# Decoder on one core: the projection's add taken earlier in three attention stages, with the order of divide, raw sums and their inverse changed in two of them

## The reference, cut to what matters

```python
x = x + L0_attn(layernorm(x), ...)     # 16 heads of 8, causal; biases, LoRA
x = x + L0_xattn(layernorm(x), ctx)    # 16 heads, 'trinity' mask; biases
x = x + L0_ffn(...)
...
x = x + L2_attn(layernorm(x), ...)     # 16 heads of 8, causal, rotary embedding, no biases
...
x = x + L3_xattn(layernorm(x), ctx, ctx, mask, ...)   # 16 heads, mask read from memory
#   ctx_ = softmax(q k^T + mask) v per head; relu(ctx_ @ wo.T + bo)
x = x + L3_ffn(...)
```

## Time and profile before

| | us |
|---|---|
| median of 3 runs | 1747.38 (1746.98 to 1747.76) |
| profiled execution, its own time | 1735.4 |
| span of the profiled execution, first to last instruction | 1733.7 |
| TensorE busy (matmuls) | 1339.4 |
| VectorE busy | 946.9 |
| ScalarE busy | 918.7 |
| GpSimd busy | 400.3 |
| mean granted clock of TensorE, share of full speed | 0.879 |

### The profile page before, as it was taken

How to read it: one execution, slowest core, us unless ns; L and a number is a source line. 1 busy time by engine, 2 the same in 40 slices (tenths; PEclk the granted TensorE clock), 3 DMA queues, 4 the chain that set the end, 5 groups by cost and what they waited for, 6 DMA issues and landing times. The chain is left out here.

```text
span 1733.7 us, 27918 instructions
## 1 busy us (share of the span) xinstructions
PE 1339.4 (77%) x9137; PEld 827.9 (48%) x9137; DVE 946.9 (55%) x3708; ACT 918.7 (53%) x2185; POOL 400.3 (23%) x490
## 2 busy tenths in 40 slices
PE   5888888868899999777996888765083577878574
PEld 3455555545444444553564555454062444444464
DVE  4577767754455555444112776647223657666432
ACT  2688877762477766532421666732020467767232
POOL 4433333210311110100004332101544042210134
PEclk9899989999999999877998898886596879989687
DMA  7900000000000000000005000000222000000012
GB/s 207 141 2 2 2 2 1 2 1 1 1 1 1 1 1 1 1 1 1 1 1 179 1 1 2 1 1 12 61 69 79 1 19 13 12 8 1 10 58 78
DMA packets 60263, 42.34 MB, mean 24 GB/s; under 512 B 13188, under 2 KB 54120, under 8 KB 60120
## 3 DMA queue, kind: packets, MB, share of 16 engines
q1 hardware_dynamic: 54752, 32.42, 7.9%
q0 software_dynamic: 3552, 7.33, 1.2%
q10 hardware_dynamic: 1816, 0.81, 0.2%
HBM read 25.88 MB, written 14.66 MB: 23 GB/s over the span
## 5 line engine op out<-in xcount | busy, mean ns | idle before, releaser
L792 ACT ACTIVATE L0a_e<-L0a_e,L0a_neg_max 128x256 f32<-128x256 f32 (+1 forms) x512 | 190.6, 447 | 19.4 <-DVE L0a_neg_max L868 19.4
L679 PE MATMUL L0a_psE<-ident,L0a_e 128*128 128x128 f32 x768 | 121.9, 288 | 16.8 <-DVE L0a_probs L877 8.2
L1216 DVE CUSTOM_DVE_ANT_0 L3x_e<-L3x_psS,L3x_mask_rows 128x256 f32<-128x256 f32 x256 | 92.9, 420 | 64.3 <-PE L3x_psS L1076 64.3
L679 PEld LDWEIGHTS L0a_psE<-ident,L0a_e 128*128 128x128 f32 x768 | 86.9, 145 | 70.5 <-issue 35.9
L1164 ACT ACTIVATE L3x_e<-L3x_e,L3x_neg_max 128x256 f32<-128x256 f32 x256 | 110.7, 503 | 12.7 <-DVE L3x_neg_max L1216 12.7
L792 ACT ACTIVATE L2a_e<-L2a_e,L2a_neg_max 128x128 f32<-128x128 f32 (+1 forms) x256 | 95.2, 445 | 33.6 <-DVE L2a_neg_max L868 33.6
L1084 PE MATMUL L3x_psE<-ident,L3x_e 128*128 128x128 f32 x512 | 81.9, 292 | 28.2 <-DVE scores_L_experts_L L1226 13.8
L868 DVE CUSTOM_DVE_ANT_0 L2a_e<-L2a_psS,causal_rows 128x128 f32<-128x128 f32 (+1 forms) x256 | 76.1, 353 | 36.9 <-PE L2a_psS L669 31.5
L868 DVE CUSTOM_DVE_ANT_0 L0a_e<-L0a_psS,trinity 128x128 f32<-128x128 f32 (+1 forms) x256 | 75.1, 352 | 37.3 <-PE L0a_psS L669 33.3
L868 DVE CUSTOM_DVE_ANT_0 L0a_e<-L0a_psS,causal_rows 128x128 f32<-128x128 f32 (+1 forms) x256 | 75.3, 352 | 35.2 <-PE L0a_psS L669 31.6
L568 POOL TENSOR_SCALAR L0a_km<-L0a_kT,quad_rows 128x256 f32<-128x256 f32 x64 | 57.9, 922 | 155.2 <-ACT L0a_kT L785 155.2
(11 more groups left out here) (652 smaller groups left out, 3231.7 us busy)
## 6 DMA issues: line engine op xcount, KB each, us to landing
L2f_rows<-packed_rows SPq DMA_DIRECT2D x8, 325.0 KB
packed_rows<-zeros SPq DMA_DIRECT2D x1, 2560.0 KB, 30.3
experts_L_L<-in_L_ffn_w_dram SPq DMA_DIRECT2D x1, 2048.0 KB, 8.4
unpacked_rows<-zeros SPq DMA_DIRECT2D x1, 2048.0 KB, 19.9
scores_L_experts_L<-in_L_ffn_w_dram SPq DMA_DIRECT2D x1, 2048.0 KB, 7.8
L2f_back_rows<-unpacked_rows SPq DMA_DIRECT2D x16, 128.0 KB, 2.5
L3x_mask_rows<-in_mask_Bx1xSxS_ff_dram SPq DMA_DIRECT2D x8, 256.0 KB, 2.7
sorted_rows<-zeros SPq DMA_DIRECT2D x1, 1472.0 KB, 19.7
```

The source lines that it names most:

```text
L679: last = nc.tensor.transpose(psE[i % 2][:, c * P:(c + 1) * P], e[:, i % RING, c * P:(c + 1) * P], mem.ident[:])
L792: last = nc.scalar.activation(at, at, ACT.Exp, bias=neg[:, i % RING, j:j + 1], scale=-1.0)
L1216: last = nc.vector.tensor_tensor_reduce(out=e[:, i % RING, j * S:(j + 1) * S], in0=psS[r][:, j * S:(j + 1) * S], in1=mrow[:, b % 2, t, :], ...
```

## The change

1. quad_heads, VectorE: `settle_x(b)` keeps only the add of the projection (and still signals s_x); it moves from n = 3 to n = 2. The statistics become `measure_x(b)`, at n = 3. 
2. masked_heads, VectorE: `settle_x(b)` keeps only the add of projection and bias into proj, signals a new semaphore s_taken, and moves from n = 3 to n = 1; TensorE's `weigh(b-1, 0)` waits for s_taken instead of s_x. The relu and the add to x, with the statistics, are `measure_x(b)` at n = 3. Before it writes proj again, settle_x waits for s_x of the bank before.
3. quad_heads: keep_raw moves from n = 7 to n = 6 (VectorE), spread_sums from n = 6 to n = 5 (TensorE), invert from n = 8 to n = 7 (ScalarE). At even n = 8 ScalarE's order was exponent(8), keep(6), invert; now it is exponent(7), invert, exponent(8), keep(6).
4. quad_heads with rope (L2a alone), GpSimd: divide(b-1) stands ahead of variants(b+2) and behind combine(b+2). L0a keeps its order.

```diff
                 for b in range(NB):
+                    if b + 2 < NB and rope:
+                        combine(b + 2)
+                    if b > 0 and rope:
+                        divide(b - 1)
                     if b + 2 < NB:
-                        if rope:
-                            combine(b + 2)
                         variants(b + 2)
                     if biased:
                         add_bias(b)
-                    if b > 0:
+                    if b > 0 and not rope:
                         divide(b - 1)
...
-                        if n == 6 and b > 0:
+                        if n == 5 and b > 0:
                             spread_sums(b - 1)
...
-                    if n == 8 and b > 0:
+                    if n == 7 and b > 0:
                         invert(b - 1)
...
                     nc.vector.tensor_tensor(xb, xb, psO[:, 0:S].rearrange("p (t d) -> p t d", t=TPB), ALU.add).then_inc(s_x, 1)
+
+                def measure_x(b):
                     dve.wait_ge(s_x, b + 1)
...
+                    if n == 2 and b >= 2:
+                        settle_x(b - 2)
                     if n == 3 and b >= 2:
-                        settle_x(b - 2)
+                        measure_x(b - 2)
...
-                    if n == 7 and b > 0:
+                    if n == 6 and b > 0:
                         keep_raw(b - 1)
...
@@ masked_heads
                         if b >= 1:
-                            pe.wait_ge(s_x, b)
+                            pe.wait_ge(s_taken, b)
...
                 def settle_x(b):
                     dve.wait_ge(s_out, b + 1)
                     dve.wait_ge(s_rows_kept, 1)
+                    if b >= 1:
+                        dve.wait_ge(s_x, b)
+                    nc.vector.tensor_tensor(proj[:], psO[:, 0:S].rearrange("p (t d) -> p t d", t=TPB),
+                                            out_bias[:].unsqueeze(1).to_broadcast([P, TPB, D]), ALU.add).then_inc(s_taken, 1)
+
+                def measure_x(b):
                     xb = mem.x[:, b * TPB:(b + 1) * TPB, :]
-                    steps.step(nc.vector.tensor_tensor(proj[:], psO[:, 0:S].rearrange("p (t d) -> p t d", t=TPB),
-                                                       out_bias[:].unsqueeze(1).to_broadcast([P, TPB, D]), ALU.add))
+                    dve.wait_ge(s_taken, b + 1)
                     nc.vector.scalar_tensor_tensor(xb, proj[:], 0.0, xb, ALU.max, ALU.add).then_inc(s_x, 1)
...
+                    if n == 1 and b >= 2:
+                        settle_x(b - 2)
                     if n == 3 and b >= 2:
-                        settle_x(b - 2)
+                        measure_x(b - 2)
```

More of the change, by code:

```diff
@@ L923, in _ @@
                 settle_x(NB - 2)
+                measure_x(NB - 2)
                 keep(LAST - 3)
@@ L927, in _ @@
                 settle_x(NB - 1)
+                measure_x(NB - 1)
 def masked_heads(nc, mem, w, name, *, wo, bo, dram_mask, probs_at):
@@ L964, in masked_heads @@
         s_raw, s_den, s_ln, s_rec = sem("raw_ready"), sem("sums_spread"), sem("log_ready"), sem("reciprocal_ready")
-        s_yT, s_out, s_x = sem("yT_ready"), sem("out_done"), sem("x_done")
+        s_yT, s_out, s_taken, s_x = sem("yT_ready"), sem("out_done"), sem("projection_taken"), sem("x_done")
         chain = sem("dve_chain")
@@ L1247, in _ @@
                         keep(i - 4)
+                    if n == 1 and b >= 2:
+                        settle_x(b - 2)
                     if n == 3 and b >= 2:
-                        settle_x(b - 2)
+                        measure_x(b - 2)
                 settle_x(B - 2)
+                measure_x(B - 2)
                 keep(LAST - 3)
@@ L1253, in _ @@
                 settle_x(B - 1)
+                measure_x(B - 1)
 def stick_heads(nc, mem, w, name, *, wq, wk, wv, wo, probs_at, scale):
```

## The result

The changed kernel takes **1664.29 us** (median of 4 runs, 1663.35 to 1666.49), the kernel before beside it 1747.47 (4 runs, 1746.98 to 1747.76): a ratio of 0.9526, 95% interval 0.951 to 0.9543, 83 us less. Predicted were 1671.7, range 1659 to 1711. (Ratios here are of the runs that were compared with each other; they can differ by 0.2% from the quotient of two medians.) The profiled execution took 1666.49 us, its span is 1664.8: 69 us less than the profiled one of before.

A forecast was written before the change was run, and what follows sets the result against it. No engine is full, so order and waits bound the kernel. Savings of 23.8 (L0a), 28.7 (L2a) and 23.2 us (L3x) sum to 75.7, about 36 waits and 40 clock; from 1747.4 that gives 1671.7 us, range 1659 to 1711.

The forecast's parts named there:

- The cycle of L0a: L0a: a loop over TensorE, ScalarE and VectorE sets bank length; banks 2 to 9 fall from 18.93 to 18.67 us.
- The price of part 3: L0a, ScalarE: the inverse ahead of item 8 costs 1.17 us on the cycle, about 0.95 from bank 10 on.
- The clock: TensorE in L0a, L2a, L3x: gaps of 2 us also lower its clock; removing them returns 40 us.
- The rule that I weighed against it: TensorE: short idles between matmul groups can still make the clock go back and forth, so its 40 us stay lost.
- Rivals B: All three stages: TensorE's clock stays as it is, only 36 us of waits go; 1711 us, chance 0.17.
- C: L0a: the new 1.4 us gap at turn 8 lowers the clock as before; about 1693 us, chance 0.15.
- D: TensorE's clock stays low for whole banks, about 13 us each; slower, 1802 us at 10 banks, chance 0.05.
- Rival E: VectorE's earlier add meets an unfinished project and holds up reduces, losing settle_x's gain; about 1725 us, chance 0.05.
- L2a: Stage L2a: earlier add and divide, inverse free; banks of 18.91 us, 28.7 us saved, 10.3 of it clock.
- L3x: Stage L3x: the weigh's 2.14 us wait goes whole; banks of 22.4 us, 23.2 us saved, some 10.4 of it clock.
- The carry: Whole kernel: the median stands 12 us above the profiled execution, so 1659.7 us becomes 1671.7 us.

The follow-up runs named there:

- Filling the gaps alone: Kernel before, order and waits unchanged, with useless matmuls on TensorE in the gaps ahead of first weighs and L2a's project: 1698.64 us, ratio 0.9769.
- Part 1 alone: Kernel before with only quad_heads' add moved to n = 2, the statistics staying at n = 3: 1659.65 us, ratio 0.9693.
- parts 3 and 4 alone: Kernel before with only the moves of keep_raw, spread_sums and invert and GpSimd's earlier divide: 1742.26 us, ratio 1.0006.
- the add at n = 1, no part 3: Changed kernel with keep_raw, spread_sums and invert moved back and quad_heads' add at n = 1: 1604.79 us, ratio 0.9372; run again, 1604.55 us, ratio 0.9373.

## Why the prediction was right

**The cycle of L0a** held to 0.04 us in all but bank 14: banks 2 to 9 took 18.64 (18.67 predicted), 10 to 13 18.24 (18.28), bank 14 17.67 (18.0). The 13 banks from 95.69 to 335.53 came to 239.84 us (240.5). The weigh waits 0.55 and turn 8 1.40, as stated.

**The price of part 3** was right: 1.17 us on the cycle predicted, 1.15 measured twice, with and without the 0.55 us gap. What I did not draw from it is that the kernel would be better without: I counted it as a term of the sum and did not ask what it bought in L2a, which the runs show to be nothing.

**The clock** was right, and it was the step with the most at stake. Filling the gaps alone took off 40.2 us in the three stages (17.1 in L0a, 10.5 in L2a, 12.6 in L3x, where the sum had 19, 10.3 and 10.4). The rule that I weighed against it (the Trainium skill, TensorE: Matmul & The Clock Gate, "A second HAM failure mode: psum-queue depth-cycling"), by which short idles would keep the clock going back and forth, is not what these banks show: with a gap of 1.40 us, one of 0.52 and one of 0.55 in each bank the granted clock was 1.00 from 75 to 350. In the same windows of the kernels that kept a gap of 1.98 us or more it was 0.86 to 0.93. The idle time of a bank in all does not tell them apart either: in bank 3 of L0a TensorE's gaps of over 0.15 us add up to 2.44 us before and to 2.46 after. It is the one long gap that has gone. Rivals B and C fall by the windows, D with them: no score of 2.09 us is left amid banks 2 to 14 of L0a. Rival E falls too: VectorE's add waits for project in none of those banks, only at the end of a stage. What in the chip tells the ones from the others no run here settles; bank 2 of the earlier trace rows, full at a gap of 1.99, is not explained by the gap's length alone.

**L2a** gave 27.8 us (28.7): banks of 18.90 (18.91), bank 6 of 17.73. By parts, 17.2 of it hang on part 4 (207.1 against 189.9), though parts 3 and 4 together, with part 1 absent, gave 10.2 only. Part 1 alone and parts 3 and 4 alone each took the stage to 207.5, all together to 190. My sum by waits would have shared it out otherwise. One reason is the clock: only together do they remove all gaps of 2 us and more. The other is that the waits overlap: a bank took 22.08 us with its gaps filled, at best 21.46 with part 1 alone and 20.34 with parts 3 and 4 alone, but 18.90 with all.

**L3x** gave 24.4 us (23.2), banks of 22.35 (22.4).

**What was mis-sized.** In L0a I had -23.8 and found -20.6. The banks are as said; the difference is the stage's two ends, which the sum had put at nothing. From the first score to the first weigh of bank 1 it took 23.8 us after and 21.3 before, because the granted clock stayed at the low level for longer (a turn at 63.98 took 1.09 us after, one at 64.69 took 0.63 before), and from the first weigh behind the last bank to the end 10.1 us after and 8.9 before. The start is not the change's doing: bank 1's weigh comes ahead of every operation that was moved, and two runs of one kernel (the add at n = 1, no part 3) took 21.3 and 23.3 us for the same stretch.

The median fell by 83.2 us, the profiled execution by 68.9, the three stages in it by 72.8 (the others were 4 us longer after). I had said that the profiled execution of before stood 12 us under its median and carried the same step over: 1659.7 to 1671.7. The profiled execution came at 1666.5, 7 us above its forecast and 2 above its median, and the median 7 us below its own. So the near hit of the median is in part luck, as two errors of opposite sign stand in it. The carry was wrong: those 12 us most likely belong to the thing that the change removes, though no slow execution of the kernel before was traced to show it. The stage code of before, run again in other kernels, took 360.2 instead of 355.2 us in L0a and 225.7 instead of 221.6 in L3x, by the clock behind the same gaps. The profiled execution seems to have been a lucky one, and a kernel without the gaps has less of such luck to lose: before ranged over 10 us in 13 runs (1735.64 to 1745.37), parts 3 and 4 alone, with more gaps, over 19 in 10, the changed kernel over 3 in 4.

**Still open.** In the later comparisons both kernels stood some 32 to 36 us lower (1711.84 and 1632.57). The three stages of the change are not where it lies: the changed kernel's took 333.5, 190.0 and 196.6 us then. It lies in the expert stages with their transfers (L2n, L2f and L3f took 46.6, 67.4 and 90.1 us in the first run, 34.1, 53.5 and 74.6 in the later one, 42 less together, while the stretches around L2f grew by 9). Why was not tried; ratios are hardly touched.

## What to carry to other kernels

When an engine waits at one fixed place in every round of a pipeline, as TensorE did here, look at what stands ahead of the awaited operation in the other engine's own list: an add of 0.4 us, parted from its statistics and moved up by one reduce, was worth 53 us (part 1 alone), and by one more another 14. Count a gap of TensorE of 2 us and more, as they stood here, at its own length and again at what the clock takes behind it; the cheapest test of the second is to fill the gap with matmuls of no use and see if the time falls. And when an operation is moved up, ask who needs it sooner: the inverse, moved up for a project that was not waiting for it, put 1.15 us on the very cycle that the rest of the change was shortening.

## What was not expected of the hardware

Matmuls of no use, added to a kernel whose order and waits stayed the same, made it 43 us faster (1698.64 against 1741.91), with TensorE's granted clock going from 0.93, 0.90 and 0.93 to 1.00 in the three windows. And the loss behind equal gaps is not a constant: with a gap of 1.99 us at the weigh bank 2 of the kernel before lost nothing and bank 3 lost 1.59 us; with one of 1.40 besides, bank 3 lost nothing and bank 4 2.83 us. With the gap of 1.40 and no longer one of 1.99, banks 2 to 14 lost nothing.
